# A causal mask moved from matrix products to a select after the exponential, and a reordered opening

## The reference

```
xn = layernorm(x)
s  = ssm(xn)      # in-projection, causal convolution of 4 taps, silu, a scan over time with 16 states,
                  # gate silu(z), out-projection
f  = ffn(xn)      # f = xn + mlp(rmsnorm(xn)), its gate modulated by attention
attention(h):     # 16 heads of 32, causal
    scores = q k^T / sqrt(32);  scores = where(causal, scores, lowest float)
    attn   = softmax(scores) v
    mod    = 0.1 * tanh((attn Wo) A)
mlp(h) = (silu(h Wg^T + (mod * (h A)) B) * (h Wu^T)) Wd^T
```

## Time and profile before

| | us |
|---|---|
| median of three runs | 2544.13 |
| lowest, highest | 2543.07, 2544.23 |
| the profiled execution | 2548.15 |
| its span, first to last instruction | 2546.1 |
| 904 to 1400, attention beside projections | 496 |
| 1404 to 1452, attention of the last sequence | 48 |

### The profile page before, as it was taken

The page is one execution under the profiler, slowest core; times in us unless marked ns, Lnnn a source line. Parts: engine busy times, 40 slices in busy tenths (PEclk is TensorE's granted clock), DMA queues, the critical chain, the costliest instruction groups (busy, mean ns, idle before and its releaser), DMA issues.

```text
span 2546.1 us, 38404 instructions
## 1 busy us (share of the span) xinstructions
PE 2479.6 (97%) x14359; PEld 1996.8 (78%) x14359; DVE 1368.0 (54%) x2860; ACT 1062.2 (42%) x1765; POOL 472.8 (19%) x430
## 2 busy tenths in 40 slices
PE   7999999999999999999999899999999999999998
PEld 5878878878778677777777678888888788888887
DVE  6856667667655588888888851221214322222323
ACT  6444544544544477777777731111112211111111
POOL 4000000000001254444443600000000202222222
PEclk9999999999999999999999999999999999999999
DMA  4000000100003776666666311111113312222212
GB/s 142 18 34 1 34 25 9 34 17 17 17 17 106 214 205 196 192 187 186 177 165 184 119 65 44 50 50 50 50 50 124 124 46 95 100 95 99 96 67 83
DMA packets 106971, 228.12 MB, mean 90 GB/s; under 512 B 14976, under 2 KB 15488, under 8 KB 100624
## 3 DMA queue, kind: packets, MB, share of 16 engines
q1 hardware_dynamic: 105056, 225.31, 27.8%
q10 hardware_dynamic: 1728, 0.29, 0.1%
HBM read 149.77 MB, written 75.50 MB: 88 GB/s over the span
## 4 chain that ended last, share of the span: by engine, by line
PE 87%; DVE 5%; issue 2%; ACT 2%; DMA 2%; SPq 1%; POOL 0%; DVEq 0%; ACTq 0%
PE PS L72 14%; PE PS L74 13%; PE PS L73 13%; PE PS L2207 4%; PE PS L2208 4%; PE PS L2209 4%; PE PS L1710 3%; PE PS L1729 3%; PE PS L1687 2%; PE PS L806 2%; PE PS L807 2%; PE PS L808 2%; PE PS L1689 2%; PE PS L1688 2%; PE PS L792 1%
## 5 line engine op out<-in xcount | busy, mean ns | idle before, releaser
L2276 DVE TENSOR_TENSOR SG<-SG,PS 128x512 f32<-128x512 f32 x124 | 85.3, 688 | 642.8 <-PE PS L74 640.9
L74 PE MATMUL PS<-FH,GU 128*128 128x512 f32 x992 | 388.3, 391 | 0.0
L72 PE MATMUL PS<-FH,GU 128*128 128x512 f32 x992 | 387.4, 390 | 0.2 <-DVE DW L2267 0.2
L73 PE MATMUL PS<-FL,GU 128*128 128x512 f32 x992 | 387.5, 391 | 0.0
L1895 DVE CUSTOM_DVE_ANT_0 PS<-PS,MK 128x512 f32<-128x512 f32 (+3 forms) x512 | 243.5, 504 | 91.4 <-PE PS L1710 90.4
L2246 ACT ACTIVATE SG<-PS 128x512 f32<-128x512 f32 x124 | 74.4, 600 | 467.3 <-PE PS L2183 467.3
L2312 POOL TENSOR_SCALAR XN<-XT,MEAN,RSTD 128x512 f32<-128x512 f32 x32 | 69.5, 2170 | 942.6 <-DMA M<-m_scratch 942.6
L1831 ACT ACTIVATE PF<-PS 128x512 f32<-128x512 f32 (+1 forms) x384 | 200.1, 526 | 83.9 <-PE PS L1731 82.0
L2249 ACT CAST GH<-SG 128x512 fp32r<-128x512 f32 x124 | 76.9, 620 | 348.2 <-DVE SG L2276 348.2
L72 PEld LDWEIGHTS PS<-FH,GU 128*128 128x128 f32 x992 | 186.4, 188 | 41.2 <-ACT SG L2246 0.6
L73 PEld LDWEIGHTS PS<-FL,GU 128*128 128x128 f32 x992 | 186.5, 188 | 41.0
(11 more groups left out here) (299 smaller groups left out, 5327.3 us busy)
## 6 DMA issues: line engine op xcount, KB each, us to landing
qk_scratch<-QT SPq DMA_DIRECT2D x128, 256.0 KB, 4.7
QS<-qk_scratch SPq DMA_DIRECT2D x96, 256.0 KB, 4.0
KS<-qk_scratch SPq DMA_DIRECT2D x96, 256.0 KB, 4.0
FH<-rh_scratch SPq DMA_DIRECT2D x16, 1024.0 KB, 5.5
FL<-rl_scratch SPq DMA_DIRECT2D x16, 1024.0 KB, 7.5
XF<-in_x_dram SPq DMA_DIRECT2D x32, 256.0 KB, 4.1
s_scratch<-ZS SPq DMA_DIRECT2D x8, 1024.0 KB, 4.3
rh_scratch<-RH SPq DMA_DIRECT2D x8, 1024.0 KB, 10.6
```

The lines of the kernel that those rows point to most:

```text
L72: pe.matmul(o, lh(k), xh(k), start=open_ and k == 0, stop=False, skip_group_check=True)
L73: pe.matmul(o, lh(k), xl(k), start=False, stop=False, skip_group_check=True)
L74: last = pe.matmul(o, ll(k), xh(k), start=False, stop=close and k == nk - 1, skip_group_check=True)
```

## The change

1. The products of `idb` and `MR` are left out. Instead keys after the query are set to 0 in PF after the exponential ("capped"), in two operations a head, each on the diagonal squares of two blocks, 256 columns: for heads 0 to 111 by Pool's `affine_select`, for the last 16 by DVE, as the minimum with CAP, a tile that is 2 where a key counts and 0 where it doesn't (an exponential is at most 1 up to rounding, since the maximum of the row is taken off).
2. ACT's cast to PH becomes a step of its own ("high") at the next head's first third, behind the next head's first exponential; it waits for both operations of "capped".
3. The remainder moves by a third, to 3g + 4, and is DVE's alone for every head, 1280 columns. Pool's part and its semaphore go.
4. In the opening ACT does `conv_open` for blocks 0 and 1 at once; slices 2 and 3 are cast in halves after blocks 0, 2, 3 and 4, and the casts of the out-projection's weights (994) move to blocks 5 and 7. Pool's parts of WL start one block later, three of them stand before its power. DVE's step 5 of the statistics moves behind BF.
5. On SP, both stores of the first sequence's rows follow relay 1; relay 2 sends out queries and keys before it fetches either. Slice 3 of the MLP's weights is loaded before the first W_down slices.

```diff
--- before
+++ after
@@ -662,6 +662,11 @@
+        def split_hi_part(act, c, half):
+            cols = slice(512 * c + 256 * half, 512 * c + 256 * half + 256)
+            act.wait_ge(s_hw[c], 16)
+            act.copy(WH[:, :, cols], W0[c][:, :, 256 * half:256 * half + 256]).then_inc(s_wh[c], 1)
@@ -676,7 +681,7 @@
             cols = slice(512 * c + 128 * m, 512 * c + 128 * m + 128)
-            pool.wait_ge(s_wh[c], 1)
+            pool.wait_ge(s_wh[c], m // 2 + 1)
             pool.tensor_tensor(WL[:, :, cols], W0[c][:, :, 128 * m:128 * m + 128], f32(WH[:, :, cols]),
@@ -993,16 +998,19 @@
-            split_hi(act, 2)
-            split_hi(act, 3)
             conv_open(0, 0)
...
+                if d in (0, 2):
+                    split_hi_part(act, 2, d // 2)
                 if d in (3, 4):
-                    out_hi(2 * d - 2, 2)
+                    split_hi_part(act, 3, d - 3)
+                if d in (5, 7):
+                    out_hi(d - 1, 2)
             act.wait_ge(s_kv, 3)
@@ -1155,7 +1163,7 @@
                 if b == 0:
-                    for step in range(2, 6):
+                    for step in range(2, 5):
                         fast_deviations(dve, 1, step)
@@ -1190,6 +1198,8 @@
                                   DTB[:, :, :].unsqueeze(2).to_broadcast([128, 4, 7, NS]), ALU.mult).then_inc(s_f, 1)
+                if b == 0:
+                    fast_deviations(dve, 1, 5)
                 dve.wait_ge(s_f, f + 6)
@@ -1262,8 +1272,8 @@
                 conv_low(pool, 0, d)
-                if d < 6:
-                    split_lo_part(pool, 2 + d // 4, d % 4)
+                if 1 <= d < 6:
+                    split_lo_part(pool, 2 + (d - 1) // 4, (d - 1) % 4)
             for b in range(NB):
@@ -1273,8 +1283,8 @@
                     pool.wait_ge(s_dt, 7)
-                    split_lo_part(pool, 3, 2)
-                    split_lo_part(pool, 3, 3)
+                    for m in range(1, 4):
+                        split_lo_part(pool, 3, m)
                     fast_powers(pool, 1)
@@ -1362,11 +1372,14 @@
+            if p == 2 and 0 <= g < HEADS:
+                at(third, "capped", g, 0)
             if p == 0 and 0 <= g - 1 < HEADS:
+                at(third, "capped", g - 1, 1)
+                at(third, "high", g - 1)
+            if p == 1 and 0 <= g - 1 < HEADS:
                 at(third, "remainder", g - 1)
-            if p == 1 and 0 <= g - 1 < HEADS - NH:
-                at(third, "remainder_end", g - 1)
             if p == 0 and 0 <= g - 2 < HEADS:
@@ -1570,8 +1583,8 @@
                 dve.tensor_copy(MK[:, 384:512], MT[0][:, :]).then_inc(a_pd, 1)
-                dve.tensor_copy(MR[:, :], MT[1][:, :]).then_inc(a_pd, 1)
-                dve.tensor_copy(idb[:, :], idn[:, :]).then_inc(a_pd, 1)
+                for c in (slice(0, 64), slice(64, 128)):
+                    dve.tensor_scalar(CAP[:, c], MT[1][:, c], 2.0, 0.0, ALU.add, ALU.max).then_inc(a_pd, 1)
                 dve.memset(BD[:, :, :], 0.0).then_inc(a_mr, 1)
@@ -1630,6 +1643,9 @@
+        def relay_back(sp, w, n):
+            r = w % 4
             if w == 1 and n == 0:
@@ -1655,10 +1671,27 @@
                         load_slice(sp, 1)
-                    relay(sp, a, how)
-                    if a < 2 and how == 1:
-                        turned_out(sp, 0, (a,))
+                    if a == 2:
+                        relay_out(sp, a, how)
+                        if how == 1:
+                            relay_back(sp, a, 0)
+                            relay_back(sp, a, 1)
+                    else:
+                        relay_out(sp, a, how)
+                        relay_back(sp, a, how)
+                    if a == how == 1:
+                        turned_out(sp, 0)
+        def capped(e, g, half):
+            P = PE_[g % 2]
+            e.wait_ge(a_ex, 3 * g + 2 + half)
+            D = P[:, 896:1152].rearrange("p (t c) -> p t c", c=128) if half else P[:, 0:1024].rearrange("p (t c) -> p t c", c=512)[:, :, 0:128]
+            if g < HEADS - NH:
+                e.affine_select(out=D, in_=D, pattern=[[0, 2], [1, 128]], compare_op=ALU.is_ge, fill=0.0, base=0,
+                                channel_multiplier=-1).then_inc(a_cp, 1)
+            else:
+                e.tensor_tensor(D, D, CAP[:, :].unsqueeze(1).to_broadcast([128, 2, 128]), ALU.min).then_inc(a_cp, 1)
@@ -1726,9 +1759,8 @@
                         n = 512 - 128 * J
-                        pe.matmul(p[:, at:at + n], KS[0:97, h, 128 * J:128 * J + 128], QS[0:97, h, 128 * J:512],
-                                  start=True, stop=False, skip_group_check=True)
-                        t = pe.matmul(p[:, at:at + 128], idb[:, :], MR[:, :], start=False, stop=True, skip_group_check=True)
+                        t = pe.matmul(p[:, at:at + n], KS[0:97, h, 128 * J:128 * J + 128], QS[0:97, h, 128 * J:512],
+                                  start=True, stop=True, skip_group_check=True)
                         at += n
@@ -1739,8 +1771,6 @@
                     pe.wait_ge(a_rm, a + 1)
-                    if a < HEADS - NH:
-                        pe.wait_ge(a_rp, a + 1)
                     for k in range(4):
@@ -1827,13 +1857,14 @@
                         act.wait_ge(a_rm, g - 1)
-                        act.wait_ge(a_rp, min(g - 1, HEADS - NH))
                     act.activation(PE_[u][:, o:o + at], PS[4 + a % 2][:, 0:at], ACT.Exp, scale=SC).then_inc(a_ex, 1)
-                    if a % 3 == 2:
-                        act.wait_ge(a_ex, a + 1)
-                        if g >= 2:
-                            act.wait_ge(a_pv, g - 1)
-                        act.copy(PH[u][:, :], PE_[u][:, :]).then_inc(a_ph, 1)
+                elif kind == "high":
+                    u = a % 2
+                    act.wait_ge(a_ex, 3 * a + 3)
+                    act.wait_ge(a_cp, 2 * a + 3)
+                    if a >= 2:
+                        act.wait_ge(a_pv, a - 1)
+                    act.copy(PH[u][:, :], PE_[u][:, :]).then_inc(a_ph, 1)
                 elif kind == "drawn":
@@ -1897,9 +1928,11 @@
                 elif kind == "remainder":
-                    u, n = a % 2, 1024 if a < HEADS - NH else 1280
+                    u = a % 2
                     dve.wait_ge(a_ph, a + 1)
-                    dve.tensor_tensor(PL[u][:, 0:n], PE_[u][:, 0:n], PH[u][:, 0:n], ALU.subtract).then_inc(a_rm, 1)
+                    dve.tensor_tensor(PL[u][:, :], PE_[u][:, :], PH[u][:, :], ALU.subtract).then_inc(a_rm, 1)
+                elif kind == "capped" and a >= HEADS - NH:
+                    capped(dve, a, how)
                 elif kind == "inverse":
@@ -1990,11 +2023,8 @@
                     pool.memset(f32(MS[:, S * a:S * a + S]), 0.0).then_inc(a_fl, 1)
-                elif kind == "remainder_end":
-                    u = a % 2
-                    pool.wait_ge(a_ph, a + 1)
-                    pool.tensor_tensor(PL[u][:, 1024:1280], PE_[u][:, 1024:1280], PH[u][:, 1024:1280],
-                                       ALU.subtract).then_inc(a_rp, 1)
+                elif kind == "capped" and a < HEADS - NH:
+                    capped(pool, a, how)
                 elif kind == "inverse":
@@ -2116,12 +2146,12 @@
             load_slice(sp, 2)
+            load_slice(sp, 3)
...
                 sp.dma_start(DST[:, n, :], wd_[n]).then_inc(m_wd, 16)
-            load_slice(sp, 3)
             for kind, n in work:
```

More of the change, by code:

```diff
@@ L1613, in prep_pool, with turned_out, relay_out @@
             pool.wait_ge(a_fl, 1)
-        def turned_out(sp, b, halves=(0, 1)):
+        def turned_out(sp, b):
             sp.wait_ge(a_rl, 4 * b + 4)
-            for half in halves:
+            for half in range(2):
                 sp.dma_start(f32((rh_d, rl_d)[half][b]), f32((RH, RL)[half][:, :, :])).then_inc(a_rst, 16)
-        def relay(sp, w, n):
+        def relay_out(sp, w, n):
             r, u = w % 4, w % 2
```

9 lines of the change are left out of this document (4 added, 5 removed).

## The result

The changed kernel takes 2615.9 us (median of 4 runs, 2613.9 to 2617.2) against 2543.6 us for the kernel before: a ratio of 1.0284, with a 95% interval from 1.0271 to 1.0296. The forecast was 2518, in a range from 2500 to 2541. The profiled execution has a span of 2611.9 us, 65.8 us more than that of before.

The account below looks back on a forecast made before the run. PE, busy 97% of the span, was taken as the bound, with DVE next. Terms: attention -25, last sequence +5, opening -4, start of attention -2, sum -26 us, from 2544.1 to 2518; range 2500 to 2541 (own range 2506 to 2531, chance 0.52).

Parts of the forecast that it names:

- PE's gain from the masks: Attention: dropping four mask products a head saves PE 0.23 to 0.48 us of its 4.58 us a head.
- Opening and start: Two terms outside the heads: 4 us saved in the opening, 2 us at the start of attention.
- the opening: Convolution before the weight casts, one VectorE step off the path: 4 us saved, 2 to 6.
- the start of attention: Sending both halves of SyncE's relay 2 at once saves 2 us, 0 to 4.
- I take 0.22, the low side: Attention, first 112 heads: net saving a head, from a range of 0.20 to 0.35; 25 us saved in all.
- the last sequence: Heads 112 to 127: two minima a head on DVE cost 5 us, between 1 and 9.
- the second select has a third (1.5 us) for itself: Attention, Pool: with ACT's cast behind the next head's first exponential, the second select has 1.5 us before the cast.
- Time enough: Attention, Pool: two selects of 0.67 us, without its remainder, make 2.57 us of work in 4.5 a head.
- The third, "slower than before": Attention: slow selects make Pool the bound from 1.73 us a select; at 2.53 us each, 2724 us; chance 0.10.
- Rival 2: Attention: selects and DVE's remainder hold each other, or ACT's cast waits for Pool; 2532 or 2538 us; chance 0.15.
- A head of 4.46 us: Sign for the forecast in the attention stretch: time a head falls from 4.68 to 4.46 us.
- ACT waiting for Pool at most heads: Sign in attention that would prove the forecast wrong, named beside selects above 1.7 us.

Follow-up runs that it names:

- no_mask_before: The kernel before without its 512 mask products and nothing in their place, against the kernel before; 2520.9 us, ratio 0.9903.
- last_masks: no_select with heads 112 to 127 given mask products on PE again and no minima on DVE; 2556.4 us, against 2567.7 without this edit.
- no_select: The changed kernel without Pool's selects for heads 0 to 111 and without ACT's wait for them; 2567.7 us, ratio 1.0096 to the kernel before.

## Why the prediction was wrong

**Right: masks and opening.** PE's gain from the masks was forecast at 0.23 us a head, 25.8 for 112; 20.6 is what 7/8 of the measured saving gives, and 23.8 what the trace of no_mask_before shows in the first heads. Opening and start were forecast at 6 us together and gave 6.6. That the sum fits is in part luck: the opening gave 5 for 4, the start of attention 0.6 for 2, and the rest is scatter. The first convolution starts at 24.5 us, even 0.7 before the forecast 25.2, since only two small operations of DVE stand before it:

```profile
24.27 0.27 DVE L1116 TENSOR_SCALAR AB_<-AB_ 128x16 f32<-128x16 f32 x1 [4.63 <-issue]
24.45 0.15 DVE L1118 TENSOR_REDUCE MB<-DB 128x1 f32<-128x8 f32 x1
24.52 0.73 DVE L1088 SCALAR_TENSOR_TENSOR XC<-PS,CW,XC 128x511 f32<-128x511 f32 x1
```

**Wrong: the remainder.** "I take 0.22, the low side, because the remainder now also starts a third later, and because the exponential that reuses its buffer, PF, waits for it." The place was named, and no price was worked out for it. The sum rested on busy time, DVE's 4.23 to 4.39 us beside PE's 4.10 to 4.35. The runs give 10 to 13 us for the extra columns (0.09 to 0.12 us a head, less than the 0.28 of DVE's work) and 29 for the third: by the traces 17.7 in the first heads, 0.16 us a head, and 8.9 in the last sequence, 0.56 a head, where the forecast had no term for it. That second term alone takes back more than the masks gave. I ought to have laid the remainder's new place, 3g+4, against its users in 3g+6: an operation of 1.5 us behind the maxima of its third, and PE in order before the values' products.

**Wrong: Pool's queue.** The step that failed is "so the second select has a third (1.5 us) for itself": in some thirds 2.5 us and more of Pool's other work stand ahead of it. "It is held where Pool is late: NU's two additions and V's two operations fall into the step just before, at about six places of a sequence. That is in the low side I took." The changed kernel has 36 such waits of the cast in seven sequences, five a sequence, so the count was right. The price was not: 44 us over about 36 places is 1.2 us at each. Moving that work took the cast's wait for Pool from 45.4 to 4.5 us and the time down by 44, so the wait went into the time almost one to one. "Time enough", 2.57 us of Pool's work in 4.5, was true of the mean and said nothing on the gap. In the rows of before Pool's other work could run late at no cost, since only its own remainder waited behind it and PE had two thirds before it needed that.

**Wrong: the last sequence.** The forecast was +5 us, at most +9. From the first exponential of head 112 to the last one the changed kernel takes 88.8 us instead of 70.0. The minima are 11 us of this by last_masks, and the later remainder some 9. The forecast priced 8 us of minima on DVE for nine heads; it took an undisturbed 0.44 us for one, where the mean is 0.71, and it had no term for the cast's wait for them, 21 us in 11 places.

**The rivals.** The third, "slower than before", had the right sign by a mechanism that did not happen: the clean select takes 0.40 us, far below the 1.73 from which Pool would be the bound. The second, selects and remainder in each other's way or the cast held by Pool, is seen: the select of 994.23 starts with a remainder and takes 1.70 us where a clean one takes 0.40. Of the 141 selects that the timeline from 904 to 1400 us lists one by one, 52 take more than 0.9 us, and each of these begins together with a remainder or during one and ends 0.3 us after it. The other way round, the remainder of 945.45 starts 0.10 us behind a select and takes 1.65 us instead of 1.49; but that is rare, and the mean is 1.52 us with selects and 1.51 without. By the rule of the Trainium skill ("SBUF — State Buffer", section "SBUF: two separate sides"), whichever of the two comes first locks the port pair for a whole instruction; the trace agrees with that. But in time the selects cost 4 us once Pool's other work is out of their way, where the rival's 2532 and 2538 lie 14 and 20 us above the forecast. In the changed kernel itself a long select also delays what stands behind it in Pool's queue; how much of the 44 us that is, the runs don't separate. What no case had is the one that came about in the first heads: every engine with room, and the results that are handed over too late in a queue. Rival 2 did name the cast's wait for Pool, but as a matter of the selects' own length.

**The signs that I named.** A head of 4.46 us, PE's idle time ended by DVE's maximum and DVE near 95% did not come: DVE was busy 404.4 of 496 us, 82%, with 68 us of waiting for PE's products. "ACT waiting for Pool at most heads" was named as a sign of being wrong; a third of the heads, 31 of 96, was enough.

## What to carry to other kernels

When an operation moves between engines, busy time per engine shows whether the work fits, not whether it is in time. For each moved result, write down the producer's queue place, what stands in that queue between it and its input, and the first user behind which others are queued; price every place in which a filler operation falls into that gap. Work that was harmless filler on a lightly loaded engine turns into delay once a hand-over of each head passes through that engine: spread it so that no two pieces meet, and give the engine only those parts whose input is ready a step early.

## What the runs showed of the hardware

Pool's select of 256 columns in place takes 0.40 us at the least and 1.76 at the most; one of 128 columns takes 0.29. The 52 over 0.9 us that the timeline lists one by one all begin with or during a remainder of DVE.

PE's granted clock was lower in the stretches with waits. In the changed kernel the products stood idle 2.08 us before 1147.65, and the stretch behind it has a granted clock of 0.58, with products of 512 columns at 0.63 us that take 0.39 otherwise:

```profile
1146.00:1150.00 4.00, 2.04 (x25) 1.47 (x26) 2.87 (x6) 2.93 (x5) 2.25 (x3) 0.99 0.50 153
1150.00:1154.00 4.00, 4.00 (x15) 3.44 (x13) 3.32 (x10) 2.58 (x5) 4.00 (x5) 0.58 0.05 14
```

```profile
1147.65 0.50 PE L1762 MATMUL PS<-QS,KS 97*128 97x512 f32 x1 [2.08 <-ACT PF L1860]
...
1149.51 0.40 PE L1721 MATMUL PS<-RL,QW 128*128 128x512 f32 x1
...
1151.51 0.63 PE L1721 MATMUL PS<-RL,QW 128*128 128x512 f32 x1
```

That is mostly the lower level, 1.2 GHz, for about 3 us of the four (an estimate from 0.58). Over 904 to 1400 us the granted clock is 0.96 where it was 1.00, and in the last sequence 0.77 (1445 to 1534 us) where it was 0.98 (1400 to 1470). So part of the loss shows as busy time of PE and not as waiting: from 904 to 1400 us PE is busy 4.44 us a head (426.1/96), and 4.23 in no_select with the same products at a clock of 0.99 (440.25/104). By that, an estimate, some 20 us of the stretch are products at the lower level. That a wait brings the lower clock about, no run shows by itself.
